# Cross attention over 1601 keys, eight batches: key projection two batches ahead, and the mask of four key tiles added by VectorE

## The chip, the cores and the metric

One Trainium2 chip, one core. The metric is the device time of one execution of the whole kernel in microseconds; the kernel is one launch that computes a four-layer network, and the change touches one function that two of its twelve parts call.

## What is computed

The stream `x` has 8 batches of 64 tokens of width 256; the context has 8 batches of 1601 rows of width 256. Two of the parts are cross attention with 16 heads of width 16, called the second and the fourth here (layers 1 and 3 in the code, tiles `l1x_` and `l3x_`):

```python
def _L1_xattn_ref(queries, keys, values, mask, W_q, W_k, W_v, W_proj, b_proj):
    Q = (queries @ W_q.T).reshape(b, sq, N_HEADS, D_HEAD).transpose(0, 2, 1, 3)   # K, V likewise, of the context
    scores = jnp.einsum('bhqd,bhkd->bhqk', Q, K) / scale
    scores = jnp.where(mask, scores, NEG_INF)
    attention = jax.nn.softmax(scores, axis=-1)
    heads_out = jnp.einsum('bhqk,bhkd->bhqd', attention, V)
    return heads_out.transpose(0, 2, 1, 3).reshape(b, sq, d) @ W_proj.T + b_proj

def _L3_xattn_ref(x, y, attn_bias, Wq, bq, Wk, Wv, Wo, bo, scale_mul_log):
    q = _l2norm(q) * scale_mul
    k = _l2norm(k)
    attn = jnp.einsum('bhqd,bhkd->bhqk', q, k) + attn_bias
    attn = jax.nn.softmax(attn, axis=-1)
    oup = jnp.einsum('bhqk,bhkd->bhqd', attn, v)
    return oup.transpose(0, 2, 1, 3).reshape(B, Lq, C) @ Wo + bo
```

The second has a mask that differs from batch to batch; the fourth has a bias that all batches share, and it normalizes each key's head vector.

## The kernel before

`context_attention` writes five instruction lists, one an engine. After a prologue that prepares batch 0, each engine runs a loop of eight iterations, one a batch. An iteration of batch b walks 13 key tiles (12 of 128 keys and one of 65): on TensorE `turned(b, m)` makes the scores of tile m, keys on partitions, in two banks; ScalarE takes the exponential of both banks (`exp`, L3595) into `pT`; TensorE's `values` (L3448) of the tile before adds up the output. Each tile has two steps, 26 in an iteration, and the list `steps` says which items of other batches' preparation every engine does in which step, between scores and values. The items:

- K (c, j): key projection of channel half c and key piece j (1024 and 577 keys), L3344. In the second, ScalarE makes the high half `kh` (L3530) and VectorE the low half `kl` (L3696). In the fourth ScalarE squares it into `sq` (L3524) and VectorE copies it to `k32` (L3692); `k32` may be written when GpSimd has split the piece of the channel half before.
- N, I, U (fourth only): the sum of squares over a head by TensorE in f32 (L3350) and VectorE's copy (L3707); logarithm and exponential on ScalarE (L3537, L3539); the product with `k32` on VectorE (L3714). Then GpSimd's `split_keys` makes `kh` and `kl` (L3271, L3273).
- V (c): value projection of four key tiles, L3360, and ScalarE's copy into `v33` (L3549).
- A (v, j): scores with queries on partitions of four heads and a quarter of the keys, L3377, from which VectorE takes the masked maxima, two instructions of L3723; 16 a batch. M (c): transposes of the maxima (L3385), put by ScalarE into row 0 of the queries (L3560), so that the scores come out shifted. The scores of a batch begin when both M are in.
- R, E, O, P: the output of the batch before (copy L3571, L3390, division, transposition L3396, projection L3401, addition L3742). O and P stand in every second batch alone.

K, N, V, A, M, E, O and P take turns on two pairs of banks (`slot`), in the order of the list: an item may start on TensorE when the item two before it has been read. `stack` on SP's queue copies `kh` and `kl` by 24 DMAs a batch (L3201) into the rows of `kst`, which has two buffers; A and the scores read it. The context's f32 rows are loaded by SP into one buffer `ctx32`, and split on GpSimd into `ctxh` and `ctxl`, one buffer each, when V of the batch before is done (L3290, L3291).

For tiles whose mask or bias TensorE adds, `turned` begins with one-hot products of 512 columns (L3425): four a tile in the second, eight in the fourth. In the fourth, tiles 0 to 3 (`ON_VECTOR`) have the bias added by VectorE instead (`add_bias`, L3754), from PSUM into `pT`, where the exponential then works in place. For such a tile the next `turned` waits for VectorE's addition, not for the exponential.

In the kernel before, all the items of iteration b, but for R, E, O and P, belong to batch b+1:

```python
    def at_step(b, s):
        of = {"R": b > 0, "E": b > 0, "O": b % 2 == 0 and b > 0, "P": b % 2 == 0 and b > 0}
        return [(it, b - 1 if it[0] in of else b + 1) for it in steps[s] if of.get(it[0], b + 1 < B)]
```

## Time and profile before

| | us |
|---|---|
| median of three runs | 2603.1 (2599.29 to 2604.42) |
| the profiled execution, its own time | 2586.07 |
| its span, first to last instruction | 2584.3 |
| TensorE busy in it | 2251.3 (87%) |
| VectorE, ScalarE, GpSimd busy | 1624.8, 1226.7, 809.8 |
| mean granted clock of TensorE | 0.952 |

The profile shows one execution. A granted clock of 1 is 2.4 GHz and 0.5 is 1.2 GHz; a figure between says how a stretch is shared between the two levels. Durations of single matmuls overlap, since they are pipelined; where a price matters, the distance from start to start is the better one. A wait names the instruction that released it.

### The profile page before, as it was taken

The numbers are of one execution on the slowest core, as the hardware profiler recorded it, in microseconds if no ns is written. First come the engines' busy times: TensorE is split into PE (matmuls) and PEld (weight loads), VectorE is DVE, ScalarE is ACT, GpSimd is POOL, SyncE is SP. The second block draws the span as 40 slices with busy tenths as digits, with TensorE's granted clock in tenths as the row PEclk, the third lists the DMA queues.
The fourth block names the chain that finished last, engine by engine and source line by source line (L and its number), as shares of the span: only waits on it lengthen the run. The fifth ranks groups of instructions, "written<-read, shape, count | busy, mean of one in ns | idle before, by whom it ended". The sixth has DMA issues, their size and how long they took to land. (4 is left out here: it accounts for less than half of the span.)

```text
span 2584.3 us, 63716 instructions
## 1 busy us (share of the span) xinstructions
PE 2251.3 (87%) x26802; PEld 1404.9 (54%) x26810; DVE 1624.8 (63%) x3620; ACT 1226.7 (47%) x2095; POOL 809.8 (31%) x655
## 2 busy tenths in 40 slices
PE   7885788888868899999999998798788888878898
PEld 6753545556534556556566655465345555555554
DVE  6976364544439846888888754545765555554577
ACT  3334144445443235555555554665345544443465
POOL 5610132422207020333322300254544343452154
PEclk9997999999989989999999999899899998888999
DMA  4203343233140256766767651232422222120132
GB/s 115 68 1 94 98 138 98 71 111 94 42 148 19 46 120 134 151 136 128 141 125 143 124 93 46 68 104 88 112 91 66 66 66 66 41 65 22 63 92 64
DMA packets 358542, 229.99 MB, mean 89 GB/s; under 512 B 289817, under 2 KB 325490, under 8 KB 358258
## 3 DMA queue, kind: packets, MB, share of 16 engines
q1 hardware_dynamic: 355186, 217.52, 34.4%
q0 software_dynamic: 3072, 8.39, 1.1%
q8 instruction: 213, 3.49, 0.6%
q14 instruction: 71, 0.58, 0.1%
HBM read 114.02 MB, written 0.52 MB: 44 GB/s over the span
## 5 line engine op out<-in xcount | busy, mean ns | idle before, releaser
L100 PE MATMUL PS<-hot 128*128 128x512 f16 x476 | 140.1, 432 | 82.3 <-DVE l0a_g L1119 17.5
L3960 POOL TENSOR_TENSOR l2x_rows<-l2x_rows,l2x_one 128x256 f16<-128x256 f32 (+1 forms) x91 | 90.9, 1025 | 377.2 <-DVE l2x_rows L1507 352.3
L4064 PE MATMUL PS<-l2x_rows,l2x_pth 128*128 128x512 f16 x832 | 200.4, 379 | 1.5 <-DVE l2x_mean L4273 1.5
L3723 DVE CUSTOM_DVE_ANT_0 l1x_junk<-PS,l1x_bias 128x401 bf16<-128x401 f32 (+1 forms) x256 | 133.1, 575 | 82.3 <-PE PS L3377 82.3
L3723 DVE CUSTOM_DVE_ANT_0 l3x_junk<-PS,l3x_bias 128x401 bf16<-128x401 f32 (+1 forms) x256 | 132.8, 574 | 49.4 <-PE PS L3377 49.2
L3595 ACT ACTIVATE l1x_pT<-PS 128x512 f32<-128x512 f32 (+1 forms) x208 | 112.7, 593 | 98.1 <-PE PS L3431 98.0
L3595 ACT ACTIVATE l3x_pT<-PS 128x512 f32<-128x512 f32 x144 | 77.8, 591 | 171.4 <-PE PS L3431 171.4
L4266 DVE TENSOR_TENSOR l2x_pl<-l2x_sc,l2x_ph 128x1664 f16<-128x1664 f32 x64 | 124.7, 1949 | 44.0 <-ACT l2x_ph L4143 43.4
L4251 DVE CUSTOM_DVE_ANT_0 l2x_sc<-PS,l2x_bias 128x1665 f32<-128x1665 f32 x64 | 120.9, 1889 | 36.3 <-issue 35.1
L4161 ACT ACTIVATE l2x_meanT<-PS 128x256 f32<-128x256 f32 x64 | 24.5, 383 | 249.8 <-PE PS L4026 249.8
L4018 PE MATMUL PS<-l2x_kh,l2x_qth 128*128 128x512 f16 (+1 forms) x512 | 132.0, 339 | 1.5 <-issue 1.5
L4018 PE MATMUL PS<-l2x_kh,l2x_qtl 128*128 128x512 f16 (+1 forms) x512 | 132.0, 339 | 0.0
L4018 PE MATMUL PS<-l2x_kl,l2x_qth 128*128 128x512 f16 (+1 forms) x512 | 132.0, 339 | 0.0
L100 PEld LDWEIGHTS PS<-hot 128*128 128x128 f16 x476 | 45.5, 107 | 154.0 <-issue 45.1
L4064 PEld LDWEIGHTS PS<-l2x_rows,l2x_pth 128*128 128x128 f16 x832 | 79.5, 98 | 72.5 <-issue 2.7
L4136 ACT ACTIVATE l2x_sc<-l2x_sc,l2x_shift 128x1665 f32<-128x1665 f32 x64 | 107.9, 1686 | 19.4 <-DVE l2x_shift L4253 19.4
L4069 PE MATMUL PS<-l2x_rows,l2x_ptl 128*128 128x256 f16 x832 | 111.6, 273 | 0.0
L4143 ACT ACTIVATE l2x_ph<-l2x_sc 128x1664 f16<-128x1664 f32 x64 | 101.8, 1591 | 8.5 <-DMA l2x_pth<-l2x_ph 6.7
L1642 POOL TENSOR_TENSOR l2f_unit_l<-l2f_unit,l2f_unit_h 128x384 f16<-128x384 f32 x72 | 75.0, 1062 | 70.5 <-ACT l2f_unit L1634 70.5
L3696 DVE SCALAR_TENSOR_TENSOR l1x_kl<-PS,l1x_kh 128x1024 f16<-128x1024 f32 (+1 forms) x32 | 31.8, 993 | 101.7 <-ACT l1x_kh L3530 101.6
L1642 POOL TENSOR_TENSOR l3f_unit_l<-l3f_unit,l3f_unit_h 128x384 f16<-128x384 f32 x68 | 73.4, 1101 | 69.7 <-ACT l3f_unit L1634 69.7
L3377 PE MATMUL PS<-l3x_kst,l3x_qst 64*64 64x401 f16 (+1 forms) x512 | 47.6, 386 | 53.5 <-DMA l3x_kst<-l3x_kh 23.4
(865 smaller groups left out, 6038.8 us busy)
## 6 DMA issues: line engine op xcount, KB each, us to landing
l2f_unit<-in_L_ffn_units_dram SPq DMA_DIRECT2D x36, 384.0 KB, 3.0
l3f_unit<-in_L_ffn_units_dram SPq DMA_DIRECT2D x34, 384.0 KB, 3.1
l1x_kst<-l1x_kh SPq DMA_DIRECT2D x128, 100.1 KB, 2.4
l3x_kst<-l3x_kh SPq DMA_DIRECT2D x128, 100.1 KB, 2.4
l2x_rows<-in_ctx_dram SPq DMA_DIRECT2D x8, 1536.0 KB
l1x_ctx<-in_ctx_t_dram SPq DMA_DIRECT2D x7, 1601.0 KB, 7.3
l3x_ctx<-in_ctx_t_dram SPq DMA_DIRECT2D x7, 1601.0 KB, 7.7
l1x_kst<-l1x_kl SPq DMA_DIRECT2D x64, 100.1 KB, 2.5
```

What stands on the lines that cost most here:

```text
L100: self.nc.tensor.matmul(self.PS[:, bank, :], self.hot[:, 0:P], self.hot[:], start=True, stop=True)
L1642: last = self.k.nc.gpsimd.tensor_tensor(wl[:, at], w[:, at], wh[:, at], ALU.subtract)
L3595: nc.scalar.activation(to, of, ACT.Exp, scale=1.0 / S_SCALE).then_inc(exp_done, 1)
L3723: last = v.tensor_tensor_reduce(junk[:, slot(it), r * BANK:r * BANK + n], PS[:, 2 * slot(it) + r, 0:n], bias[:, 0 if normed else b % 2, at ...
L3960: last = nc.gpsimd.tensor_tensor(high[:, at], of[:, at], one[0:p, at].unsqueeze(2).unsqueeze(3).to_broadcast([p, i, NC, P]), ALU.mult)
L4018: last = nc.tensor.matmul(PS[:, j, 0:n], x[:, d, r, :], y[:, b % 2, d, at:at + n], start=(e == 0), stop=(e == len(terms) - 1))
L4064: nc.tensor.matmul(PS[:, ACC, :], pth[:, u % 2, m, :], rows2[:, b % 2, :, :, m, :], start=(m == 0), stop=False)
L4069: last = nc.tensor.matmul(PS[:, ACC, 0:D], ptl[:, u % 2, m, :], rows2[:, b % 2, 0, :, m, :], start=False, stop=(m == KT - 1))
L4136: nc.scalar.activation(sc[:], sc[:], ACT.Exp, bias=shift[:, u % 2:u % 2 + 1], scale=1.0 / S_SCALE, accum_out=rsum[:, u % 4:u % 4 + 1]).the ...
L4143: nc.scalar.activation(ph[:], sc[:, 0:ODD], ACT.Copy).then_inc(p_high, 1)
L4251: link(v.tensor_tensor_reduce(sc[:], PS[:, 0:len(cols), :].rearrange("p b n -> p (b n)")[:, 0:KEYS], bias[:], 1.0, LOWEST, ALU.add, ALU.ma ...
L4266: v.tensor_tensor(pl[:], sc[:, 0:ODD], ph[:], ALU.subtract).then_inc(p_low, 1)
```

## The change

The steps are written anew for both layers. V now stands first, A follows, and K (with N, I and U) comes from step 14 on and belongs to batch b+2, so that keys are stacked an iteration before they are asked for. Iteration 0 has lists of its own (`opening_steps`, `second_keys`): there batch 1 is prepared as before and the keys of batch 2 as well. SP's order of stacking, context and mask loads follows; the context is split in two pieces of keys, so that K of the first piece needn't wait for the second. In the second layer tiles 0 to 3 are added to `ON_VECTOR`: a second mask with keys on partitions is loaded (from a host copy in that layout, 832 bytes a partition), turned into 0 and a large negative number by GpSimd, and added by VectorE.

```diff
--- before.py
+++ after.py
@@ -3010,7 +3010,7 @@
     NEAR = 4.0
     MASKED = -2.0 ** 30
     ONE_HOT = 2.0 ** 6 if normed else 1.0
-    ON_VECTOR = list(range(4)) if normed else []
+    ON_VECTOR = list(range(4))
 
     def vector_count(b, m, g):
 
@@ -3021,29 +3021,45 @@
 
     A = [("A", v, j) for v in range(QV) for j in range(NCH)]
     R_, E, O_, P_ = ("R", 0, 0), ("E", 0, 0), ("O", 0, 0), ("P", 0, 0)
+    K_ = [("K", c, j) for c in range(NC) for j in range(NH)]
+    N_ = [("N", c, j) for c in range(NC) for j in range(NH)]
+    I_ = [("I", c, j) for c in range(NC) for j in range(NH)]
+    U_ = [("U", c, j) for c in range(NC) for j in range(NH)]
+    V_ = [("V", c, 0) for c in range(NV)]
+    M_ = [("M", c, 0) for c in range(2)]
     if normed:
-        steps = [[("K", 0, 0)], [("K", 0, 1)], [("N", 0, 0), R_], [("N", 0, 1), ("I", 0, 0)], [("U", 0, 0), ("I", 0, 1), ("V", 0, 0)],
-                 [E, ("U", 0, 1)], [("V", 1, 0)], [("K", 1, 0)], [("K", 1, 1)],
-                 [O_, ("N", 1, 0)], [("N", 1, 1), ("I", 1, 0)], [("U", 1, 0), ("I", 1, 1), ("V", 2, 0)],
-                 [P_, A[0], ("U", 1, 1)], [A[1], A[2]], [("V", 3, 0)], [A[3], A[4]], [A[5]], [A[6]], [A[7], A[8]],
-                 [A[9]], [("M", 0, 0), A[10]], [A[11]], [A[12], A[13]], [A[14], A[15]], [("M", 1, 0)], []]
+        steps = [[V_[0]], [], [R_, V_[1]], [], [E], [V_[2]], [V_[3]], [O_], [A[0]], [A[1], A[2]], [A[3]], [A[4]], [P_, A[5]], [A[6], A[7]],
+                 [K_[0]], [K_[1], A[8]], [N_[0], M_[0]], [N_[1], I_[0], A[9]], [U_[0], I_[1], A[10]], [U_[1], K_[2], A[11]],
+                 [K_[3], A[12]], [N_[2], A[13]], [N_[3], I_[2], A[14], A[15]], [U_[2], I_[3]], [U_[3]], [M_[1]]]
+        opening_steps = [[K_[0]], [K_[1]], [N_[0]], [N_[1], I_[0]], [U_[0], I_[1], V_[0]], [U_[1], K_[2]], [K_[3], V_[1]], [N_[2]],
+                         [N_[3], I_[2], V_[2]], [U_[2], I_[3]], [U_[3], V_[3]], [], [], [], [], [],
+                         [A[0], A[1]], [A[2], A[3]], [A[4]], [A[5], A[6]], [A[7], A[8]], [A[9], A[10]], [M_[0], A[11]],
+                         [A[12], A[13]], [A[14], A[15]], [M_[1]]]
+        second_keys = {18: [K_[0]], 19: [K_[1]], 20: [N_[0]], 21: [N_[1], I_[0]], 22: [U_[0], I_[1], K_[2]], 23: [U_[1], K_[3]],
+                       24: [N_[2]], 25: [N_[3], I_[2], U_[2], I_[3], U_[3]]}
     else:
-        steps = [[("K", 0, 0)], [], [("K", 0, 1), R_], [("K", 1, 0)], [E], [("K", 1, 1)], [("V", 0, 0)], [O_], [A[0]], [A[1]],
-                 [("V", 1, 0), A[2]], [A[3]], [P_, A[4]], [("V", 2, 0), A[5]], [A[6]], [A[7]], [("V", 3, 0), A[8]], [A[9]],
-                 [("M", 0, 0), A[10]], [A[11]], [A[12]], [A[13]], [A[14]], [A[15]], [("M", 1, 0)], []]
+        steps = [[V_[0]], [], [R_], [V_[1]], [E], [V_[2]], [V_[3], A[0]], [O_, A[1]], [A[2], A[3]], [A[4]], [A[5]], [A[6]], [P_, A[7]],
+                 [A[8]], [K_[0]], [A[9], M_[0]], [A[10]], [K_[1]], [A[11]], [A[12]], [K_[2]], [A[13]], [A[14]], [A[15], K_[3]], [],
+                 [M_[1]]]
+        opening_steps = [[K_[0]], [], [K_[1]], [K_[2]], [], [K_[3]], [V_[0]], [], [V_[1]], [], [V_[2]], [V_[3]], [], [A[0]], [A[1], A[2]],
+                         [A[3], A[4]], [A[5], A[6]], [A[7], A[8]], [A[9], A[10]], [M_[0], A[11]], [], [A[12]], [A[13]], [A[14]], [A[15]],
+                         [M_[1]]]
+        second_keys = {20: [K_[0]], 22: [K_[1]], 23: [K_[2]], 25: [K_[3]]}
-    assert len(steps) == STEPS
+    assert len(steps) == len(opening_steps) == STEPS
     WARM = 3
     OFF_SLOT = "IUQTRFZY"
 
     def at_step(b, s):
-        of = {"R": b > 0, "E": b > 0, "O": b % 2 == 0 and b > 0, "P": b % 2 == 0 and b > 0}
-        return [(it, b - 1 if it[0] in of else b + 1) for it in steps[s] if of.get(it[0], b + 1 < B)]
+        if b == 0:
+            return [(it, 2) for it in second_keys.get(s, [])] + [(it, 1) for it in opening_steps[s]]
+        of = {"R": b - 1, "E": b - 1, "O": b - 1, "P": b - 1, "K": b + 2, "N": b + 2, "I": b + 2, "U": b + 2}
+        return [(it, of.get(it[0], b + 1)) for it in steps[s] if of.get(it[0], b + 1) < B and (it[0] not in "OP" or b % 2 == 0)]
 
     prepared = [(it, 0) for it in first]
     tail = [(R_, B - 1), (E, B - 1), (O_, B - 1), (P_, B - 1)]
@@ -3101,8 +3117,7 @@
         kst = sb("kst", [P, 2, R, NK], F16)
         v33 = sb("v33", [P, 2, KT, H, VW])
         bias = sb("bias", [P, 1 if normed else 2, NK], BF16)
-        if normed:
-            bias_t = sb("bias_t", [P, len(ON_VECTOR), S])
+        bias_t = sb("bias_t", [P, 1, len(ON_VECTOR), S]) if normed else sb("bias_t", [P, 2, KT, S], BF16)
         one_hot = sb("one_hot", [P, BANK], F16 if normed else BF16)
         junk = sb("junk", [P, 2, BANKS], BF16)
         rmax = sb("rmax", [P, 2, QV, NCH])
@@ -3137,6 +3152,7 @@
             q_scale = sb("q_scale", [P, H])
         else:
             mask8 = sb("mask8", [P, NK], U8)
+            mask_t = sb("mask_t", [P, KT, S], U8)
             every = sb("every", [P, NT, NK], U8)
             alive = sb("alive", [P, NT])
 
...
@@ -3189,6 +3205,7 @@
                     for half in range(2):
                         sp.dma_start(mask8[half * S:(half + 1) * S, :],
                                      ins["mask_Bx1xSxS2_bk0"][b].rearrange("a s n -> (a s) n")).then_inc(bias_loaded, 16)
+                    sp.dma_start(mask_t[:], ins["mask_columns"][b]).then_inc(bias_loaded, 16)
 
                 def stack(b, c):
 
@@ -3205,18 +3222,28 @@
                     load_mask(0)
                 sp.dma_start(w[:, 3, :, :], ins[L + weight["o"] + "_heads"].rearrange("g p n -> p g n")).then_inc(loaded["rest"], 16)
                 sp.dma_start(b_o[:], row(ins[L + ("bo" if normed else "b_proj")]).to_broadcast([P, D])).then_inc(loaded["rest"], 16)
-                for b in range(B):
-                    if b + 1 < B:
-
-                        sp.wait_ge(ctx_parts, FIRST_CTX + b)
-                        sp.dma_start(ctx32[:], ins["ctx_t"][b + 1].rearrange("(c p) n -> p c n", p=P)).then_inc(ctx_loaded, 16)
-                        if not normed:
-                            sp.wait_ge(bias_made, b + 1)
-                            load_mask(b + 1)
-                    stack(b, 0)
-                    stack(b, 1)
+                def load_ctx(b):
+
+                    sp.wait_ge(ctx_parts, FIRST_CTX + NH * (b - 1))
+                    sp.dma_start(ctx32[:], ins["ctx_t"][b].rearrange("(c p) n -> p c n", p=P)).then_inc(ctx_loaded, 16)
+
+                load_ctx(1)
+                for c in range(NC):
+                    stack(0, c)
+                if not normed:
+                    sp.wait_ge(bias_made, 1)
+                    load_mask(1)
+                load_ctx(2)
+                for b in range(B - 1):
+                    for c in range(NC):
+                        stack(b + 1, c)
+                    if b + 2 < B and not normed:
+                        sp.wait_ge(bias_made, b + 2)
+                        load_mask(b + 2)
+                    if b + 3 < B:
+                        load_ctx(b + 3)
                 if later is not None:
-                    sp.wait_ge(ctx_parts, FIRST_CTX + B - 1)
+                    sp.wait_ge(ctx_parts, FIRST_CTX + NH * (B - 1))
                     later.load(sp)
 
             @block.gpsimd
@@ -3256,8 +3283,10 @@
                     pool.wait_ge(bias_loaded, (b + 1) * BIAS_LOADS)
                     if b >= 2:
                         pool.wait_ge(turned_made, (b - 1) * STEPS)
+                        pool.wait_ge(biased, vector_count(b - 1, 0, 0))
                     hold()
-                    nc.gpsimd.tensor_scalar(bias[:, b % 2, :], mask8[:], -MASKED, MASKED, ALU.mult, ALU.add).then_inc(bias_made, 1)
+                    link(nc.gpsimd.tensor_scalar(bias[:, b % 2, :], mask8[:], -MASKED, MASKED, ALU.mult, ALU.add))
+                    nc.gpsimd.tensor_scalar(bias_t[:, b % 2, :, :], mask_t[:], -MASKED, MASKED, ALU.mult, ALU.add).then_inc(bias_made, 1)
                     pool.wait_ge(bias_made, b + 1)
 
                 def split_keys(b):
@@ -3287,9 +3316,12 @@
                     pool.wait_ge(ctx_loaded, b * 16)
                     pool.wait_ge(made, number[(LAST_USE, b - 1)] + 1)
                     hold()
-                    link(nc.gpsimd.tensor_tensor(ctxh[:], ctx32[:], one[:].unsqueeze(2).to_broadcast([P, NC, NK]), ALU.mult))
-                    nc.gpsimd.tensor_tensor(ctxl[:], ctx32[:], ctxh[:], ALU.subtract).then_inc(ctx_parts, 1)
-                    pool.wait_ge(ctx_parts, FIRST_CTX + b)
+                    for h, (at, n) in enumerate(halves):
+                        link(nc.gpsimd.tensor_tensor(ctxh[:, :, at:at + n], ctx32[:, :, at:at + n],
+                                                     one[:].unsqueeze(2).to_broadcast([P, NC, n]), ALU.mult))
+                        nc.gpsimd.tensor_tensor(ctxl[:, :, at:at + n], ctx32[:, :, at:at + n], ctxh[:, :, at:at + n],
+                                                ALU.subtract).then_inc(ctx_parts, 1)
+                        pool.wait_ge(ctx_parts, FIRST_CTX + NH * (b - 1) + h + 1)
                     if normed:
                         split_keys(b)
                     else:
@@ -3337,7 +3369,7 @@
                             pe.wait_ge(w_parts, 1)
                             pe.wait_ge(ctx_parts, j + 1)
                         else:
-                            pe.wait_ge(ctx_parts, FIRST_CTX + b)
+                            pe.wait_ge(ctx_parts, FIRST_CTX + NH * (b - 1) + j + 1)
                         for i, at, n in pieces(*halves[j]):
                             terms = [(x, y, d) for x, y in ((wh, ctxh), (wh, ctxl), (wl, ctxh)) for d in range(NC)]
                             for m, (x, y, d) in enumerate(terms):
@@ -3750,8 +3782,11 @@
                         dve.wait_ge(summed, e - 2 * G2 + 1)
                     to = pT[0:n, (b * KT + m) % 2, g, :].rearrange("p (u s) -> p u s", s=S)
                     of = PS[0:n, S_BANK + g, :].rearrange("p (u s) -> p u s", s=S)
-                    each = bias_t[0:n, m, :].unsqueeze(1).to_broadcast([n, BANK // S, S])
-                    v.scalar_tensor_tensor(to, each, S_SCALE, of, ALU.mult, ALU.add).then_inc(biased, 1)
+                    each = bias_t[0:n, 0 if normed else b % 2, m, :].unsqueeze(1).to_broadcast([n, BANK // S, S])
+                    if normed:
+                        v.scalar_tensor_tensor(to, each, S_SCALE, of, ALU.mult, ALU.add).then_inc(biased, 1)
+                    else:
+                        v.tensor_tensor(to, of, each, ALU.add).then_inc(biased, 1)
 
                 for it in prepared:
                     item(it)
@@ -4431,6 +4466,7 @@
     a["L3_xattn_scale_mul_log_row"] = a.pop("L3_xattn_scale_mul_log").reshape(H)
     tiled = lambda v: np.ascontiguousarray(np.moveaxis(columns(v), 0, -3).swapaxes(-1, -2))
     a["fside_columns"] = tiled(a["fside_SxS2_0"])
+    a["mask_columns"] = tiled(a["mask_Bx1xSxS2_bk0"][:, 0])
     n = np.arange(D)
     turns = 2.0 * np.pi * (np.outer(n, n) % D) / D
     a["dft_cos"] = np.cos(turns).astype(np.float32)
```

## Rows read from the trace of the kernel before

**Rows 1.** The page, busy time: us, share of the span, instructions.

```profile
PE 2251.3 (87%) x26802; PEld 1404.9 (54%) x26810; DVE 1624.8 (63%) x3620; ACT 1226.7 (47%) x2095; POOL 809.8 (31%) x655
```

**Rows 2.** Windows, second cross attention by iteration: us, busy of each engine, PEclk, DMA.

```profile
373.50:418.50 45.00, 39.80 (x1046) 26.07 (x1046) 21.27 (x74) 23.11 (x45) 12.75 (x5) 1.00 0.23 58
...
661.30:709.60 48.30, 42.19 (x1086) 27.64 (x1086) 22.10 (x77) 23.86 (x49) 0.86 (x1) 1.00 0.22 54
709.60:737.45 27.85, 20.39 (x918) 14.48 (x918) 0.50 (x2) 15.28 (x31) 0.00 (x0) 0.97 0.02 4
sum 363.95, PE 315.04 PEld 205.66 DVE 153.33 ACT 180.35 POOL 81.63; mean PE 39.38 PEld 25.71 DVE 19.17 ACT 22.54 POOL 10.20
```

**Rows 3.** Windows, fourth cross attention by iteration, same columns.

```profile
1879.70:1938.70 59.00, 49.41 (x1070) 30.39 (x1074) 34.64 (x90) 29.80 (x52) 26.00 (x15) 0.93 0.32 98
...
2249.30:2314.00 64.70, 54.10 (x1135) 32.62 (x1130) 36.36 (x93) 30.78 (x56) 20.56 (x13) 0.90 0.23 65
2314.00:2345.70 31.70, 24.94 (x962) 17.86 (x954) 5.55 (x10) 16.04 (x32) 15.03 (x3) 0.82 0.02 4
sum 466.00, PE 388.30 PEld 240.10 DVE 254.70 ACT 228.64 POOL 190.74; mean PE 48.54 PEld 30.01 DVE 31.84 ACT 28.58 POOL 23.84
```

**Rows 4.** Waits from 1880 to 2345: total us, times, longest.

```profile
PE PS L3377 <- DMA l3x_kst<-l3x_kh: 23.4, 7, 4.0
```

**Rows 5.** Timeline of TensorE, fourth: start, us, what, idle before it.

```profile
2046.00 0.54 PE L3377 MATMUL PS<-l3x_kst,l3x_qst 64*64 64x401 f16 x8 [2.46 <-DMA l3x_kst<-l3x_kh]
2046.47 0.92 PE L3448 MATMUL PS<-l3x_pT,l3x_v 128*17 128x64 f32 x32
```

**Rows 6.** Windows, ten microseconds of a later batch of the fourth.

```profile
2170.00:2180.00 10.00, 8.03 (x170) 4.20 (x170) 5.28 (x21) 2.99 (x7) 5.26 (x1) 0.51 0.58 180
```

**Rows 7.** Timeline of TensorE, second: a key tile with V between.

```profile
482.17 0.41 PE L3425 MATMUL PS<-l1x_one_hot,l1x_bias 64*64 64x512 bf16 x4
482.41 0.42 PE L3431 MATMUL PS<-l1x_qst,l1x_kst 64*64 64x64 f16 x32
...
485.40 0.38 PE L3396 MATMUL PS<-ident,l1x_o 128*128 128x128 f32 x2
485.71 0.64 PE L3448 MATMUL PS<-l1x_pT,l1x_v 128*17 128x64 f32 x32
```

**Rows 8.** Timelines of TensorE, ScalarE and VectorE, second: K and its copies.

```profile
469.39 0.61 PE L3344 MATMUL PS<-l1x_ctxh,l1x_wh 128*128 128x512 f16 x2
...
472.20 1.02 ACT L3530 ACTIVATE l1x_kh<-PS 128x1024 f16<-128x1024 f32 x1 [1.60 <-PE PS L3344]
...
473.25 1.23 DVE L3696 SCALAR_TENSOR_TENSOR l1x_kl<-PS,l1x_kh 128x1024 f16<-128x1024 f32 x1 [7.89 <-ACT l1x_kh L3530]
```

**Rows 9.** Groups from 1830 to 2360: VectorE's maxima and mask additions.

```profile
L3723 DVE CUSTOM_DVE_ANT_0 l3x_junk<-PS,l3x_bias 128x401 bf16<-128x401 f32 (+1 forms) x256 | 132.8, 574 | 49.4 <-PE PS L3377 49.2
...
L3754 DVE SCALAR_TENSOR_TENSOR l3x_pT<-l3x_bias_t,PS 128x512 f32<-128x512 f32 x64 | 41.0, 681 | 42.5 <-PE PS L3431 42.5
```

**Rows 10.** Timeline of TensorE, fourth: the norm products of a channel half.

```profile
2005.44 3.01 PE L3350 MATMUL PS<-l3x_sq,l3x_ones 128*128 128x512 f32 x8
```

**Rows 11.** Timelines of GpSimd and VectorE, fourth: a split and the product beside it.

```profile
2012.40 1.88 POOL L3271 TENSOR_TENSOR l3x_kh<-l3x_k,l3x_one 128x1024 f16<-128x1024 f32 x1
2014.36 2.54 POOL L3273 TENSOR_TENSOR l3x_kl<-l3x_k,l3x_kh 128x1024 f16<-128x1024 f32 x1
...
2013.23 1.67 DVE L3714 TENSOR_TENSOR l3x_k<-l3x_k,l3x_n 128x577 f32<-128x577 f32 x1 [0.32 <-ACT l3x_n L3539]
```

**Rows 12.** Timeline of TensorE, second: scores of the last, partial tile.

```profile
513.04 2.21 PE L3431 MATMUL PS<-l1x_qst,l1x_kst 64*64 64x64 f16 x32
```

**Rows 13.** Timeline of TensorE, fourth, last iteration: two tiles in a row.

```profile
2327.83 0.63 PE L3425 MATMUL PS<-l3x_one_hot,l3x_fsp 64*64 64x512 f16 x8 [0.62 <-ACT l3x_pT L3595]
...
2329.90 0.63 PE L3425 MATMUL PS<-l3x_one_hot,l3x_fsp 64*64 64x512 f16 x8 [0.62 <-ACT l3x_pT L3595]
```

**Rows 14.** Timeline of SP's queue, fourth: issues of stacking DMAs.

```profile
2020.83 1.24 SPq L3201 DMA_DIRECT2D l3x_kst<-l3x_kh  x2
```

4 lines of the change are left out of this document (2 added, 2 removed).

## The prediction

> **What bounds it now.** I read the page first: TensorE is busy for 87% of the span [rows 1], so an edit pays where TensorE stands still or runs at its lower clock. The change touches two layers of the same function, the second cross attention ("second": no key norm) and the fourth ("fourth": with it). I cut both loops into iterations, one per batch, at the ScalarE copy of the row maxima (L3560) that ends each. The second takes 363.95 us for eight iterations, the fourth 466.0 [rows 2, 3]: together a third of the kernel. In the second, iterations 1 to 5 (the sum less the first and the last two) are 363.95 - 45.0 - 48.3 - 27.85 = 242.8 us (48.6 each), TensorE busy 42 of 48 in the one shown, at the full clock. In the fourth they are 466.0 - 59.0 - 64.7 - 31.7 = 310.6 (62.1 each), TensorE busy 49 to 54 in the rows shown, the granted clock 0.90 to 0.93 there and 0.82 in the last.
>
> Then the waits of TensorE. Only the fourth has a big one: score products (L3377) waiting for the key rows that SP's DMAs stack, 23.4 us in 7 waits, one a batch [rows 4]. Its surroundings are as important: it ends at 2046.00, and the values products behind it take 0.92 us where the same 32 take 0.64 at the full clock [rows 5, 7]; in another batch the same phase has a stretch granted 0.51 [rows 6], almost all 1.2 GHz. By the granted clock an iteration spends 2 x (1 - clock) of its time at 1.2 GHz: 0.14, 0.20 and 0.36 in the iterations shown [rows 3]. The second layer has no DMA wait and hardly any of this.
>
> **The change, part by part.** Prices, all by start to start in the timelines: a key tile's scores are 0.24 (bias products, L3425) + 0.35 in the second [rows 7]; V 2.64 us [rows 7]; K of 1024 keys 2.7, its copy on ScalarE 1.0, its low half on VectorE 1.25, so K's pair of banks is free 2.5 us after K ends [rows 8]; a mask addition on VectorE 0.68, a chunk of maxima (A) two of 0.57, which in the timeline start 0.5 apart, so 1.0 an A [rows 9]; the norm product N of a channel half 3.0 [rows 10]; GpSimd's split of a 1024-key piece 4.6, of 577 keys in proportion 2.6; VectorE's 577-wide product beside it 1.67 [rows 11]; the last, partial tile 2.8 to 3.4, as its 1-row weights take 2.2 us [rows 12]; a tile with nothing between its parts 2.07 [rows 13]; the issue of a stacking DMA 0.6 [rows 14]. With these I walk each instruction list in order, each engine in order, each item waiting for the release of its bank pair two items before. Check of the method: the old steps 0 to 5 of the second come out at 13.1 us; the rows give 482.17 - (469.39 - 0.59) = 13.4 [rows 7, 8]. It is 1 to 2% short.
>
> *Mask on VectorE (second only).* Per batch 4 tiles lose 16 bias products, 4 x 0.24 = 1.0 us of TensorE. VectorE gets 8 additions, 8 x 0.65 = 5.2 us, on 22 busy of 48: there is room. But ScalarE's exponentials start one addition later, and the V copy queued behind them in tile 3 too. GpSimd makes a second mask of 832 columns (under the 1.88 us that 1024 columns take [rows 11]) at the start of an iteration, where it idles, and SP issues one more DMA of 0.6: covered, and worth no more than that if uncovered.
>
> *Steps rearranged, second.* V in steps 0 to 6, A0 at 6, K from 14. Ends of tiles, from the iteration's start: tile 3 at 15.5, tile 6 at 23.6, tile 9 at 35.0, tile 11 at 44.8, tile 12 and the maxima at 49.5; without the output items (odd batches) 47.8. TensorE's waits in it: O behind V3's late copy 1.8; M0, which has K0's banks, 2.2 (2.5 less A9's 0.3); A14 behind K2 0.95; A15 0.6; K3 0.7; the copy of the maxima 1.9. Taking 1% on, 5 iterations are 2 x 50 + 3 x 48.3 = 245, with some 3 us of clock 248, against 242.8: +5.
>
> *Ends, second.* Iteration 0 now also makes the keys of batch 2 in steps 20 to 25 (+8.2 us of K, and their waits): the walk gives 54.7 for 45.0. Iteration 6 makes none: 38.8 for 48.3. Zero in sum.
>
> *Steps rearranged, fourth.* The stacking DMAs of batch b+1 no longer follow K by a few steps. They are issued from the end of iteration b-1 (kst is free when batch b-1's scores are done): 12 of 0.6 us [rows 14] for the first half, so heads 0 and 1 are issued at 3.8 and landed by 6.5 us, the last by 17; A0 asks at 13.5, A8 at 29. The DMA wait goes: -3.3 us a batch. On SP only the context load for b+3 stands behind them. But K2's copy on VectorE (step 19) must wait for GpSimd's split of the first piece, since both use k32: U0 ends at 15.5 of the second part, the split at 20.0, K2's copy at 21.2; queued behind K2 on VectorE is A11, and TensorE has nothing it may do, as K3 has K2's banks: an idle of 2.65 us. Before, V and the output items lay there. With 1.2 each before N1 and N2 and 2.0 at the end the second part (steps 14 to 25) is 36.6, the first 23.0 (21.5 in odd batches): 59.6 and 58.1. Five iterations, 1% on: 296.5; at the old rate of clock losses about 307, at full clock 296.5. The A chunks now lie between dense 512-column products, as in the second, where the clock holds; I take 301.5: -9.
>
> *Ends, fourth.* Iteration 0 has both key sets; the second's U0, I1 and K2 stand in one step (22), and K2 waits 4.7 us for GpSimd with A11 behind it: the walk gives 85 for 59.0, +26. Iteration 6 loses 14 us of K and N and all their waits, 40.5 for 64.7: -24. The last one, begun at the low clock before (0.82), -1.5. Sum +0.5, taken as 0 to +1.
>
> Context halves: the same work of GpSimd in two parts. At 4.4 us for 1024 columns [rows 11] it is 9 us for the first half and 14 in all, from V3 at 12 on; K0 asks at 24, K1 at 26.5. Covered, except in iteration 0 of the fourth, where the walk has 1.4 and 1.3 us for it.
>
> **Sum.** Second +5, fourth -9 + 0.5: about -4 us. The profiled execution is 2586.1 (span 2584.3, 1.8 around it), 17 below the median of 2603.1; the sum would make it 2582, and the median 2599. Each walk can be wrong by 1 us a batch either way (10 to 12 us in both layers).
>
> **Rivals.**
> A. *The clock recovers in the fourth.* Its eight iterations spend some 84 us at 1.2 GHz (2 x (1 - clock) x time, added over all eight, of which three are shown [rows 3]); products done in it took twice their time. For: the low stretches follow the DMA wait and the run of small products. Against: a 2.65 us idle takes its place. If it holds the full level, iterations 1 to 5 give 296.5 - 310.6 = -14, the low clock of the old ends -5, the second +5, and 4 of the percents put on go: -18, 2585.
> B. *The wait is exchanged and keeps the clock low (slower).* Place: K3 in step 20, every batch, and 5 us in iteration 0. The old wait of 2.5 us was enough for the lower level [rows 5]; the new one is as long, and behind it stand K3 and N2, 3.4 us of dense work, and the two tiles, which TensorE and not VectorE bounds. At 1.2 GHz that adds 3.5 us, 2.2 more than the 1.3 that I put down for the old stretch [rows 5]; six times +13, the fourth otherwise at its old losses 307 - 310.6 = -4, the second +5: +14, 2617. It decides if the low level follows K3's wait in three or more batches. The Trainium skill (TensorE: Matmul & The Clock Gate, "HAM oscillation") says that a wait recurring in every round of a loop can put the array back to the half clock each round, which speaks against this change if the new wait recurs. By it the time is B's.
> C. *The second layer gains after all.* If the V copies and M0 wait less than walked, the 1.0 us of bias products is kept: -3 in place of +5: 2591. For: its TensorE idles 6 of 48 us, so any order has room. Against: M0 after K0 in the same banks is fixed by the list.
> D. *The transfers stay late:* SP would have to come to stack(b+1) after 10 us, held by the context load that waits for GpSimd. That wait ends at 26 us of the iteration before, so this is unlikely; then the 23.4 us [rows 4] stay beside the new wait, 2622.
>
> **How the numbers follow.** A measurement of this kernel can tell about 0.2%, 5 us, from no change. Forecast 0.36 (2594 to 2604), A 0.24, B 0.22, C 0.14, D 0.04. Faster: A, most of C and 0.06 of the forecast, 0.42. Same: 0.30 and the rest of C, 0.32. Slower: B and D, 0.26. The range holds the forecast with its 10 to 12 us of error, and A and B but for their outer tails: 2578 to 2620.
>
> **What would show it.** Right: no wait of L3377 for the kst DMAs; in the fourth a wait of L3344 of 2 to 3 us in each iteration 1 to 5, released by VectorE's k32 copy (L3692), and that copy's wait now naming GpSimd's split; iterations of 58 to 61 us; iteration 0 over 80, iteration 6 near 40. In the second, a wait before L3385 of about 2 us, iterations of 48 to 50, bias products 288 in place of 416. Wrong: if the granted clock in the fourth is 0.98 (A) or under 0.90 (B), or the second's iterations are at 46 (C).

## The result, and the profile after

| | before | after |
|---|---|---|
| median, us | 2603.4 (2599.29 to 2604.42, 4 runs) | 2637.7 (2625.72 to 2645.39, 4 runs) |
| the profiled execution, and its span | 2586.07, 2584.3 | 2635.16, 2633.4 |
| ratio, 95% interval | | 1.0131 [1.009, 1.0172] |

The change makes the kernel 1.3% slower, 34 us. I had put 2599 first and 2578 to 2620 as the range; the time lies outside it, on the side of rival B, and above B's 2617.

The same windows as in [rows 2] and [rows 3], each from one ScalarE copy of the row maxima to the next. First the second cross attention of the changed kernel (us, busy of each engine, PEclk, DMA share, GB/s):

```profile
389.60:447.90 58.30, 49.39 (x1074) 30.06 (x1078) 29.51 (x88) 26.75 (x48) 14.42 (x8) 0.94 0.30 82
447.90:496.60 48.70, 40.15 (x1084) 26.07 (x1070) 27.14 (x86) 24.07 (x47) 13.53 (x8) 1.00 0.32 90
496.60:547.40 50.80, 41.73 (x1070) 27.21 (x1070) 26.73 (x85) 24.63 (x49) 14.88 (x9) 1.00 0.33 90
547.40:602.70 55.30, 44.48 (x1072) 27.94 (x1064) 26.39 (x84) 24.01 (x46) 14.86 (x9) 0.91 0.29 82
...
654.10:708.10 54.00, 45.33 (x1064) 28.21 (x1064) 26.40 (x84) 24.04 (x47) 14.87 (x9) 0.87 0.21 54
708.10:746.20 38.10, 32.46 (x1022) 22.87 (x1022) 22.63 (x77) 21.23 (x44) 1.81 (x2) 1.00 0.27 68
...
sum 385.60, PE 317.15 PEld 204.84 DVE 191.10 ACT 185.46 POOL 89.34; mean PE 39.64 PEld 25.60 DVE 23.89 ACT 23.18 POOL 11.17
```

and the fourth:

```profile
1915.20:2008.60 93.40, 70.44 (x1146) 39.04 (x1146) 45.46 (x105) 40.23 (x65) 33.07 (x23) 0.89 0.24 68
...
2068.50:2132.70 64.20, 54.47 (x1122) 32.83 (x1122) 35.09 (x93) 31.01 (x57) 26.38 (x18) 0.92 0.24 66
2132.70:2191.10 58.40, 48.99 (x1116) 30.06 (x1116) 34.86 (x92) 30.46 (x54) 26.27 (x18) 1.00 0.26 73
...
2317.60:2363.50 45.90, 39.83 (x1058) 26.31 (x1058) 22.86 (x77) 20.89 (x45) 26.90 (x8) 0.89 0.32 91
2363.50:2394.70 31.20, 23.58 (x938) 16.37 (x938) 5.55 (x10) 15.98 (x31) 0.00 (x0) 0.89 0.01 4
sum 479.50, PE 393.96 PEld 239.00 DVE 251.01 ACT 230.70 POOL 193.74; mean PE 49.25 PEld 29.88 DVE 31.38 ACT 28.84 POOL 24.22
```

Both layers lost: the second 385.6 for 363.95, the fourth 479.5 for 466.0. The iterations differ between executions by a few us, through the clock. Three profiled executions of the changed kernel (two are the controls below) and two of the one before give, us:

| | second before | second after | predicted | fourth before | fourth after | predicted |
|---|---|---|---|---|---|---|
| iteration 0 | 45.0, 45.0 | 58.3, 58.8, 58.3 | 54.7 | 59.0, 58.2 | 93.4, 98.4, 97.4 | 85 |
| 1 to 5, sum | 242.8, 243.7 | 260.2, 260.6, 260.5 | 248 | 310.6, 313.3 | 309.1, 309.5, 306.9 | 301.5 |
| iteration 6 | 48.3, 48.3 | 38.1, 39.6, 40.3 | 38.8 | 64.7, 64.9 | 45.9, 44.2, 46.9 | 40.5 |
| iteration 7 | 27.9, 27.9 | 29.0, 29.7, 29.6 | 27.9 | 31.7, 32.1 | 31.2, 32.6, 31.8 | 30.2 |

By the means: second +13.5 +17.2 -9.0 +1.5 = +23; fourth +37.8 -3.5 -19.1 +0 = +15; together +38, where the medians differ by 34.

One pair of profiles can mislead here by several us. Some kernels of the next section leave one of the two layers in its old form or in its changed one, and their profiles give more executions of each (second, old: the kernel before, h1, e2, f3, f4, g2, g3; changed: the changed kernel, g1, h2, e1; fourth, old: the kernel before, h1, e1, e3, e4, f1, f2, h3; changed: the changed kernel, g1, h2, e2). By the means, the second's loop takes 365.5 us over seven executions of the old form and 389.1 over four of the changed one, +23.6; the fourth's takes 471.6 over eight and 481.0 over four, +9.4. The sum, +33, is that of the medians. By iterations:

| | second before | second after | change | fourth before | fourth after | change |
|---|---|---|---|---|---|---|
| iteration 0 | 45.2 | 58.6 | +13.4 | 59.4 | 96.2 | +36.8 |
| 1 to 5, sum | 241.9 (238.8 to 243.9) | 261.1 (260.2 to 263.2) | +19.2 | 315.3 (310.6 to 318.5) | 307.7 (305.5 to 309.4) | -7.6 |
| iteration 6 | 49.6 | 39.9 | -9.7 | 65.0 | 45.3 | -19.7 |
| iteration 7 | 28.9 | 29.5 | +0.6 | 31.9 | 31.8 | -0.1 |

The waits of TensorE. In the second, iterations 1 to 5 (total us, times, longest):

```profile
PE PS L3417 <- DVE l1x_ticks L3731: 11.0, 5, 2.2
PE PS L3409 <- DVE l1x_rmax L3755: 10.1, 17, 1.0
PE PS L3409 <- DVE l1x_ticks L3731: 6.4, 9, 1.0
```

In the fourth, iterations 1 to 5, and then iteration 0:

```profile
PE PS L3376 <- DVE l3x_k L3724: 14.0, 5, 2.8
PE PS L3409 <- DVE l3x_rmax L3755: 7.4, 10, 1.0
PE PS L3382 <- DVE l3x_ticks L3741: 6.1, 5, 1.2
PE PS L3382 <- DVE l3x_k L3724: 5.7, 5, 1.2
...
PE PS L3409 <- DVE l3x_k L3724: 7.0, 3, 3.6
PE PS L3409 <- DVE l3x_ticks L3741: 2.8, 3, 1.1
PE PS L3376 <- POOL l3x_ctxl L3322: 2.5, 1, 2.5
```

L3417 are M's transposes, L3409 the maxima products, L3376 K, L3382 N, L3724 VectorE's copy to `k32`, L3731 and L3741 its releases of banks behind K and N, L3755 its maxima. The 23.4 us of [rows 4] are gone: no score product waits for a DMA. In their place stands what the prediction named: M0 waits 2.2 us behind K0 in the second, K3 2.8 us behind K2's copy in the fourth, each in every batch. And VectorE's copy itself waits for GpSimd's split (L3302), 15.4 us over the fourth in this row of the groups:

```profile
L3724 DVE TENSOR_SCALAR l3x_k<-PS 128x1024 f32<-128x1024 f32 (+1 forms) x32 | 31.2, 991 | 61.0 <-ACT l3x_sq L3556 45.5 <-POOL l3x_kl L3302 15.4
```

### The profile page after: what moved, and what is told of

Read it like the earlier page. It is cut to its first block and busy times, and to the rows that moved or that the text cites. A ratio compares the mean times of both kernels' runs of the same rounds, so it can differ in the third digit from the quotient of the medians.

```text
span 2633.4 us, 63574 instructions
## 1 busy us (share of the span) xinstructions
PE 2265.6 (86%) x26674; PEld 1403.9 (53%) x26682; DVE 1658.2 (63%) x3684; ACT 1234.6 (47%) x2095; POOL 818.8 (31%) x691
## 5 line engine op out<-in xcount | busy, mean ns | idle before, releaser
L3755 DVE CUSTOM_DVE_ANT_0 l1x_junk<-PS,l1x_bias 128x401 bf16<-128x401 f32 (+1 forms) x256 | 132.1, 574 | 30.2 <-PE PS L3409 29.4
L3755 DVE CUSTOM_DVE_ANT_0 l3x_junk<-PS,l3x_bias 128x401 bf16<-128x401 f32 (+1 forms) x256 | 132.6, 574 | 25.8 <-PE PS L3409 24.6
L3627 ACT ACTIVATE l1x_pT<-PS 128x512 f32<-128x512 f32 x144 | 78.1, 594 | 89.2 <-PE PS L3463 89.0
L4171 ACT ACTIVATE l2x_sc<-l2x_sc,l2x_shift 128x1665 f32<-128x1665 f32 x64 | 107.9, 1686 | 19.5 <-DVE l2x_shift L4288 19.4
L3280 POOL TENSOR_TENSOR l3x_tick<-ones 1x1 f32<-1x1 f32 x39 | 10.9, 281 | 259.0 <-DVE l3x_k L3746 214.0
L4104 PEld LDWEIGHTS PS<-l2x_rows,l2x_ptl 128*128 128x128 f16 x832 | 81.6, 98 | 15.6
```

What stands on the lines that cost most here:

```text
L3627: nc.scalar.activation(to, of, ACT.Exp, scale=1.0 / S_SCALE).then_inc(exp_done, 1)
L3755: last = v.tensor_tensor_reduce(junk[:, slot(it), r * BANK:r * BANK + n], PS[:, 2 * slot(it) + r, 0:n], bias[:, 0 if normed else b % 2, at ...
L4104: last = nc.tensor.matmul(PS[:, ACC, 0:D], ptl[:, u % 2, m, :], rows2[:, b % 2, 0, :, m, :], start=False, stop=(m == KT - 1))
L4171: nc.scalar.activation(sc[:], sc[:], ACT.Exp, bias=shift[:, u % 2:u % 2 + 1], scale=1.0 / S_SCALE, accum_out=rsum[:, u % 4:u % 4 + 1]).the ...
```

## The experiments

The two layers share one function, so each can have its own copy of it. Each was timed in five rounds, `h1` and `h2` in three, against the kernel before on the same chip.

**One layer at a time, one part of the second at a time.** `e1_second_only` has the changed function in the second layer and the old one in the fourth, `e2_fourth_only` the reverse. `e3_mask_only` is the kernel before but for the second's mask on VectorE (`ON_VECTOR`, `bias_t`, `mask_t`), `e4_second_steps` has the second's new lists, context halves and DMA order, without that mask.

> The second layer as after the change, the fourth as before. Theory W (waits written into the new lists, made larger by the lower clock): the second's loop takes 386 us in place of 364, its five middle iterations 51 to 55 where TensorE's clock falls, and the kernel is 18 to 24 us slower than before. Rival P (the loss is not of the lists: 16 us of the profiled difference lie in the first layer, where nothing was changed, in gaps of TensorE that no wait explains): the second's loop still takes 386, but whether the kernel is 20 or 36 us slower depends on whether those gaps in the first layer come with this program too. Rival M (VectorE's mask additions are what costs): as W here; the mask-only kernel parts them.

> The fourth layer as after the change, the second as before. Theory W: the fourth's loop takes about 480 us in place of 466, all of it in iteration 0 (93 for 59) less what iteration 6 gives back (46 for 65), so the kernel is 10 to 15 us slower. Rival P: the loop's time in the timed runs is equal to before, and what differs lies in the first layer.

> The old lists and order of loads; in the second layer alone the mask of key tiles 0 to 3 by VectorE. Theory W: 1 us a batch less on TensorE (32 groups of four bias products, 0.24 us each, 8 us in all), part of it lost to the later exponentials: 0 to 8 us faster than before. Rival M: the longer chain of scores, addition, exponential costs 1 to 2 us in each batch, 8 to 16 us slower.

> The second layer with the new lists and order of loads, its whole mask by TensorE as before; the fourth as before. Theory W: 18 to 30 us slower, as the second-only kernel or some us more, since the lists carry the loss. Rival M: no slower than before by more than 5 us.

| | median, us | ratio, 95% interval | changed loop, us |
|---|---|---|---|
| e1_second_only | 2614.56 | 1.0090 [1.0066, 1.0113] | second 393.2 |
| e2_fourth_only | 2595.11 | 1.0027 [1.0009, 1.0045] | fourth 477.0 |
| e3_mask_only | 2593.09 | 1.0004 [0.9988, 1.0020] | second 368.2 |
| e4_second_steps | 2610.65 | 1.0080 [1.0062, 1.0098] | second 384.5 |

The kernel before had 2590.94 here. The second layer is the larger loss, 23.6 us, the fourth 4 to 7 (less than the 10 to 15 I expected); together 1.0117, inside the whole change's interval. In the second the loss is in the new order of steps (1.0080 of 1.0090): the mask alone neither gives nor takes, though it removes 128 bias products, some 8 us of TensorE by my price. So rival C had nothing to keep: that gain doesn't show with the old order either.

**The controls.** In its profiled execution the changed kernel came to the second's loop 16 us later than the kernel before (389.6 for 373.5), with idles of TensorE in the first layer that no code of the change touches:

```profile
41.55 0.58 PE L423 MATMUL PS<-l0x_w_kvh,l0x_rh 128*128 128x256 f16 x2 [5.20 <-issue]
```

Is it the program or the occasion (all that was measured together, on one chip)? `g1_control` is the changed kernel again; `h1_before_again` and `h2_after_again` are both kernels, unaltered, on one chip.

> The changed kernel again, nothing altered. Its profiled run lost some 16 us in the first layer, in gaps of TensorE that the profile calls issue, before either changed loop. If that belongs to the program, the second's loop starts again at 388 to 391 us and the two halves alone (+0.9% and +0.27%) fall short of the whole: ratio 1.015 to 1.018. If it belongs to that one execution, the loop starts at 371 to 378, the span is near 2615, and the ratio is the sum of the halves, 1.0117 (1.009 to 1.014).

> The kernel before, unaltered, with a profile, on the same occasion as the next run. In some profiled runs, whatever the kernel's first layer, TensorE loses 13 to 16 us before 60 us; the occasions that show it have the kernel before at 2603 and 2607 us, those that don't at 2591 and 2592. If the loss goes with the occasion, both runs of this pair show the second's loop start at the same time, 371 to 378 or 385 to 392. If it goes with the program, this one starts at 371 to 378 and the next at 388 to 392. Ratio 1.000 (0.998 to 1.002).

> The changed kernel, unaltered, beside the kernel before on the same occasion. By the occasion theory its second loop starts where that of the run before starts, within 3 us, and the ratio is 1.012 to 1.015. By the program theory it starts 13 to 16 us later than the run before, at 388 to 392.

g1: 2644.77, ratio 1.0145 [1.0121, 1.0169], its second loop from 391.1; that is the start I expected if the loss was the program's, and a ratio between my two expectations. h1: 2606.83, 1.0004 [0.9983, 1.0024]. h2: 2639.91, 1.0127 [1.009, 1.0164]. The windows from 20 to 60 us, first the profiled kernel before, then h1, then h2:

```profile
20.00:60.00 40.00, 36.94 (x292) 30.05 (x291) 26.92 (x48) 14.94 (x32) 31.50 (x30) 0.93 0.33 95
```

```profile
20.00:60.00 40.00, 30.02 (x197) 21.16 (x195) 18.21 (x31) 9.99 (x21) 29.84 (x29) 0.83 0.32 91
```

```profile
20.00:60.00 40.00, 27.38 (x168) 18.25 (x167) 16.20 (x29) 8.42 (x17) 28.80 (x29) 0.78 0.33 94
```

The kernel before, unaltered, gets through 197 matmuls there instead of 292 and comes to the second's loop at 385.1 instead of 373.5. So most of the 16 us belongs to the occasion. h2 starts 7.3 us later still, at 392.4, where I had asked for 3; but two programs that are the old one up to that loop (g2 and g3 below) start at 391.8 and 385.7 on such an occasion. Whether a part of these 7 us is the program's stays open. The occasion explains the kernel before too: it had 2603 beside the first profile of the changed kernel (389.6) and 2607 in both groups (g, h) whose profiled kernels start at 385 to 392, 2591 and 2592 in both (e, f) whose kernels start at 371 to 378; its first profile, 2586 and 17 below its own median, is of the early kind. Each of the groups e, f, g and h was measured on a chip of its own, so these runs can't tell the chip from the occasion. Each ratio is taken on one chip and hardly feels it: the changed kernel has 1.0131, 1.0145 and 1.0127 where profiles start late, and its two halves, measured where they start early, add up to 1.0117.

**The second: wait or clock?** e1's iterations 1 to 5 are granted 0.88 to 0.97 and take 263.2 us. Three kernels go out from e1. `f1_keys_end_tile` puts M0 ahead of K0, so that it doesn't wait for K0's banks, and one more item of maxima, A13, ahead of K2:

```diff
-[A[8]], [K_[0]], [A[9], M_[0]], [A[10]], [K_[1]], [A[11]], [A[12]], [K_[2]], [A[13]], [A[14]],
+[A[8]], [A[9]], [M_[0], K_[0]], [A[10]], [K_[1]], [A[11]], [A[12]], [A[13]], [K_[2]], [A[14]],
```

`f2_dense_in_maxima` adds idle-filling products, whose result nobody reads, ahead of A0 to A7:

```diff
+                        if b > 0 and c < 2:
+                            k.warm(bank, 2)
```

`h3_spread_values` moves V3 in among the maxima, packs K closer and, as f1, puts M0 ahead of K0:

```diff
-[E], [V_[2]], [V_[3], A[0]], [O_, A[1]], [A[2], A[3]], [A[4]], [A[5]], [A[6]], [P_, A[7]], [A[8]], [K_[0]], [A[9], M_[0]], ...
+[E], [], [V_[2], A[0]], [O_, A[1]], [A[2]], [V_[3], A[3]], [A[4]], [A[5]], [P_, A[6]], [A[7]], [A[8]], [A[9]], [M_[0], K_[0]], ...
```

> As the second-only kernel (0.9% slower than before), but in the second's steps 14 to 23 K stands last in its tile: A9 and then M0, K0; A12, A13 and then K2. Theory W (the waits written into the list are part of the loss): the 2.2 us wait of the maxima transposes behind K0 and the 1.0 of A14 behind K2 go, 2 to 3 us in each of iterations 1 to 5, and the low clock at 30 us of the iteration with them: 10 to 18 us less than the second-only kernel, 0.2 to 0.5% slower than before. Rival C (the clock in the run of small products is the loss, these waits are not): less than 5 us gained.

> As the second-only kernel, with two products of 128x512 that nothing reads put in front of each of the first eight chunks of maxima in the second's loop (into the chunk's own bank, which it then overwrites): 3.5 us a batch more work for TensorE. Rival C (TensorE falls to 1.2 GHz in the run of small products that waits for VectorE, and pays for it in the dense work that follows): the clock stays at its full level at 15 to 24 us of the iterations and the loop is 3 to 10 us shorter, or at least no longer, in spite of 24 us of added products. Theory W (only the waits themselves): the added products fill VectorE's time at best, the loop stays within 3 us, and is up to 15 us longer if they do not fit.

> The second layer's change alone, with values products V3 moved in among the first maxima (step 9) and the keys packed closer (steps 16, 18, 20, 23, with M0 ahead of K0). Theory that the lower clock in the bare run of maxima is what the walk missed: time at the lower clock in iterations 1 to 5 falls from 28 to 36 us to under 20, and these iterations take 247 to 252, ratio 1.001 to 1.004. Rival, the maxima wait for VectorE whatever lies between them, and the order only moves the wait: idle of TensorE stays at 41 to 45, iterations 255 to 260, ratio 1.005 to 1.008.

Iterations 1 to 5 of the second. Idle is the length less TensorE's busy time, and at 1.2 GHz is 2 x (1 - clock) x length, added up:

| | ratio, 95% interval | length | busy | idle | at 1.2 GHz |
|---|---|---|---|---|---|
| before, h1 | 1, 1.0004 | 242.8, 243.7 | 212.7, 214.1 | 30.1, 29.6 | 13.8, 17.1 |
| changed, three times | 1.0131, 1.0145, 1.0127 | 260.2, 260.6, 260.5 | 214.5, 216.9, 216.5 | 45.7, 43.7, 44.0 | 27, 34, 31 |
| e1 | 1.0090 [1.0066, 1.0113] | 263.2 | 219.1 | 44.1 | 36 |
| f1 | 1.0050 [1.0028, 1.0072] | 254.9 | 213.2 | 41.7 | 31.1 |
| f2 | 1.0134 [1.0113, 1.0156] | 262.9 | 227.2 | 35.7 | 7.5 |
| h3 | 1.0078 [1.0053, 1.0103] | 253.1 | 209.9 | 43.2 | 9.2 |

f2, then h3, in two of their windows:

```profile
482.20:536.40 54.20, 46.98 (x1086) 28.91 (x1086) 27.09 (x85) 24.70 (x49) 14.89 (x9) 0.97 0.30 84
536.40:587.90 51.50, 44.28 (x1080) 27.14 (x1080) 26.68 (x84) 24.07 (x47) 14.91 (x9) 1.00 0.32 89
```

```profile
449.30:498.70 49.40, 40.74 (x1083) 26.31 (x1069) 27.36 (x86) 23.88 (x46) 13.45 (x8) 1.00 0.32 89
498.70:549.40 50.70, 42.21 (x1070) 27.13 (x1070) 26.91 (x85) 24.47 (x48) 14.84 (x9) 1.00 0.32 90
```

In these profiles both restore the clock and neither restores the time. f2 pays for it in products: in its profile the iterations take 262.9 us for e1's 263.2. That profile is f2's fastest execution, 2613.87 at a clock of 0.953; the other four had 0.940 to 0.952 and took 2618 to 2629, so the 7.5 us are not those of the ratio, 1.0134. Either way filling the idle is no cure. h3 brings the time at 1.2 GHz under that of the kernel before and keeps the idle at 43.2 us: the clock theory had the time of the low stretches right (under 20) and the length wrong (253 for 247 to 252; 1.0078 for at most 1.004), the rival the idle right (41 to 45). What is left at the full clock is waits. M0's and A14's are a real part: f1, which moves both, takes 8.3 us off e1's iterations 1 to 5 (263.2 to 254.9) and 0.4% off the time. Which of the two gives it was not parted, and the low clock, which I expected to go with them, stays (31 us for 36). M0's wait goes and others take some of its place: K waits 13.2 us there for VectorE (L3755, L3731), 3.0 in the changed kernel.

**The fourth.** Two kernels go out from e2. `f3_second_half_later` moves K2 and K3 one step later, behind A12 and A13, and with them N2 and N3, so that GpSimd has split the first piece by then; `f4_opening` spreads the maxima of iteration 0 from step 13 on instead of 16 and puts K2 and K3 of the second key set into step 24.

```diff
-[U_[1], K_[2], A[11]], [K_[3], A[12]], [N_[2], A[13]], [N_[3], I_[2], A[14], A[15]], [U_[2], I_[3]], [U_[3]], [M_[1]]
+[U_[1], A[11]], [A[12], K_[2]], [A[13], K_[3]], [N_[2], A[14]], [N_[3], I_[2], A[15]], [U_[2], I_[3]], [U_[3], M_[1]]
```

Two more take K2's wait for GpSimd away by a second buffer, in the space of `xn` and `xnT`, which nobody reads any more: `g2_k32_twice` is e2 with it, `g3_k32_twice_opening` f4 with it. `g4_both_amended` is the whole change, with f1's order in the second and g3's fourth.

```diff
-            k32 = sb("k32", [P, NK])
+            k32_both = sb("k32", [P, NK]), x_both
...
+                            k32 = k32_both[c if b > 0 else 0]
                             if x >= NH:
-                                dve.wait_ge(key_low, x - NH + 1)
+                                back = NH if b == 0 or (b == 1 and c == 0) else NC * NH
+                                dve.wait_ge(key_low, x - back + 1)
```

> As the fourth-only kernel (0.27% slower than before), but K of the second channel half comes one to two steps later in the steady iterations (steps 20 and 21, N in 22 and 23), after more chunks of maxima. Theory W (VectorE's copy of K2 waits for GpSimd's split, and K3 waits for it, 2.8 us in each of five iterations): that wait falls under 1 us, 1.5 to 3 us less in each of iterations 1 to 5, 8 to 14 us in all, so 0.1 to 0.3% faster than before. Rival E (the wait only moves to N2, N3 and the end of the iteration): within 4 us of the fourth-only kernel.

> As the fourth-only kernel, but in iteration 0 the chunks of maxima begin at step 13 in place of 16, and the second key set's K2 and K3 stand in step 24, two steps after U0, in place of 22 and 23. Theory W (iteration 0 pays for two key sets with waits of TensorE of 3.6, 2.5, 2.2 and 2.1 us for k32 and for the context split): 5 to 10 us less in iteration 0 (95.5 in the fourth-only kernel), the rest the same, so about equal to before. Rival E: iteration 0 stays over 92, the waits going to N2 and N3 in the last step.

> The fourth layer's change alone, with a second k32 (in the space of xn and xnT, free by then), so that the unit keys of the second channel half do not wait for GpSimd's split of the first. Theory of the exchanged wait: the idle before K3 (2.8 us, iterations 1 to 5) and the 4.5 us in iteration 0 go, 12 to 18 us less than the fourth's change alone: ratio 0.996 to 0.998, iterations 1 to 5 at 58 to 59. Rival, the run of small products and not the wait holds the lower clock and VectorE and ScalarE are next in line: K2's squares on ScalarE and the norm products bring their own waits, 3 to 6 us less, ratio 1.000 to 1.002.

> As the run before, with the order of iteration 0 in which the maxima are spread from step 13 and K2, K3 of the second key set share step 24. The opening order alone was worth 0.3% with one k32. If its gain was the same wait for GpSimd, the two do not add up: ratio within 0.001 of the run before. If it was the spreading of the maxima, they add: another 3 to 8 us, ratio 0.993 to 0.996.

> The whole change with all three amendments: second layer with the key products at the ends of tiles, fourth with two k32 and the spread opening. If the layers add up, the ratio is that of the run before plus 0.005: 0.998 to 1.002, against 1.0131 for the change as made. If it is over 1.004, the layers disturb each other.

| | ratio, 95% interval | it. 0 | 1 to 5 | it. 6 | fourth's loop |
|---|---|---|---|---|---|
| e2_fourth_only | 1.0027 [1.0009, 1.0045] | 95.5 | 305.6 | 44.2 | 477.0 |
| f3_second_half_later | 1.0128 [1.0105, 1.0151] | 98.3 | 330.5 | 41.1 | 501.7 |
| f4_opening | 0.9993 [0.9978, 1.0008] | 90.8 | 310.3 | 44.2 | 477.2 |
| g2_k32_twice | 0.9928 [0.9906, 0.9950] | 89.9 | 292.3 | 47.0 | 460.9 |
| g3_k32_twice_opening | 0.9930 [0.9909, 0.9950] | 84.7 | 291.0 | 44.8 | 452.0 |
| g4_both_amended | 0.9996 [0.9978, 1.0015] | 84.2 | 294.2 | 45.5 | 455.4 |

f3 missed widely: 8 to 14 us less was expected, and by the ratios it takes 26 us more than e2. Its waits of K in iterations 1 to 5 are two, not one:

```profile
PE PS L4163 <- DVE l3x_rmax L4542: 12.0, 5, 2.4
PE PS L4169 <- DVE l3x_ticks L4528: 11.7, 10, 1.2
PE PS L4163 <- DVE l3x_k L4511: 10.2, 5, 2.1
```

(K is L4163 here, N L4169.) K2's and K3's waits for the split shrink from 2.8 to 2.1 us a batch, but K2 now follows A12 in the pairs of banks and waits 2.4 for VectorE's maxima, and N2, N3 and U stand on the iteration's end, where N waits 11.7 us for the banks (6.1 in e2) and the scores 9.3 us in five waits that the profile gives no releaser. To move the waiting item added waits.

g2 is the decisive one. The first rows of its waits in iterations 1 to 5 (K is L4165, A L4198, N L4171; `x_both` is the second buffer), and two of its windows:

```profile
PE PS L4198 <- DVE l3x_rmax L4547: 7.4, 10, 1.0
PE PS L4171 <- DVE l3x_x_both L4515: 6.2, 5, 1.2
PE PS L4171 <- DVE l3x_ticks L4532: 6.1, 5, 1.2
PE PS L4165 <- DVE l3x_x_both L4515: 3.5, 5, 0.7
```

```profile
1987.20:2043.60 56.40, 48.99 (x1116) 30.06 (x1116) 37.33 (x93) 30.55 (x55) 28.33 (x19) 1.00 0.18 54
...
2043.60:2103.20 59.60, 51.91 (x1118) 32.21 (x1122) 35.08 (x93) 30.99 (x57) 26.36 (x18) 0.96 0.26 71
```

K3's wait falls from 13.9 us in e2 to 3.5, the five iterations from 305.6 to 292.3 (13.3 less, 2.7 each), iteration 0 by 5.6, and the kernel is 0.7% faster than before. The two ratios differ by 0.0099, 26 us, with intervals of 0.002 each; the layer's loops by 16, in one execution each. I expected 12 to 18 us, ratio 0.996 to 0.998; where the rest of the 26 comes from stays open. f4's opening order takes 4.7 us off iteration 0; its loop as a whole doesn't show it (477.2), the ratio does by 0.3%. With two buffers the ratio doesn't change (0.9930 for 0.9928), while in the profiles iteration 0 is 5.2 us shorter again; the intervals are too wide for 5 us, so whether the opening order's gain was the same wait is not shown. g2 and g3 are the fastest of all; g4 gives back the 0.5 to 0.7% that the new order in the second costs.

## Why the prediction was wrong, step by step

The waits and their sizes were right: no DMA wait; K3 idle 2.8 us in each of five batches (2.65 predicted), released by the copy of `k32`, which waits for GpSimd; M0 2.2 us (2.2); bias products of the second 288. The test of doing without the K3 wait took 10.4 us of wait and 13.3 of time from five iterations.

**The step that failed is the term for the clock.** The prediction walked at the full clock and added the lower clock as "some 3 us" in the second, 5 in the fourth and nothing in the iterations at the ends, on the ground that the second layer has "hardly any of this". Iterations 1 to 5 of the new order measured 12.7 us over their own full-clock time in the second and 12 over the walk in the fourth, and the fourth's iteration 0 spent 21 to 37 us at 1.2 GHz. The old times on the other side of the comparison held such losses too, 6.8 us in the second's iterations 1 to 5, and were set against the walk as they were. Part by part:

**Second, iterations 1 to 5: +5 predicted, +17 measured (+19 over all executions).** At the full clock the walk holds within 1%: iterations granted 1.00 take 48.7 (odd) and 50.8 (even) for 48.3 and 50. But the 242.8 on the other side hold some low clock themselves: at 1.00 the old order takes 46.6 and 48.3 (46.5 and 46.6 in h1, 46.8 and 48.3 in the profile before), which makes 3 x 46.6 + 2 x 48.3 = 236.4. Against it the new order has 3 x 48.7 + 2 x 50.8 = 247.7: +11.3, where the prediction's own 245 against 236.4 would have been +8.6. I had called 48.6 an iteration "at the full clock" from the one window shown, and walked only steps 0 to 5 of the old list, never the whole. The clock is the rest: 260.4 - 247.7 = 12.7 us for 243.2 - 236.4 = 6.8, 6 us more (I had put 3 in all). Two of the old odd iterations at the full clock, from h1 and from the profile before:

```profile
526.50:573.10 46.60, 40.76 (x1080) 26.82 (x1080) 21.77 (x76) 23.48 (x47) 13.64 (x6) 1.00 0.34 97
```

```profile
614.50:661.30 46.80, 40.73 (x1080) 26.80 (x1080) 21.85 (x76) 23.41 (x47) 13.58 (x6) 1.00 0.33 95
```

The low clock lies at the start of iterations, and in iteration 5 also in the run of maxima and about M0's and K3's waits. V0 of iteration 2, at the full clock, and of iteration 3, at 1.2 GHz:

```profile
497.82 0.39 PE L3392 MATMUL PS<-l1x_wh,l1x_ctxh 128*128 128x256 f16 x2
498.05 0.38 PE L3392 MATMUL PS<-l1x_wl,l1x_ctxh 128*128 128x256 f16 x2
...
548.81 0.61 PE L3392 MATMUL PS<-l1x_wh,l1x_ctxh 128*128 128x256 f16 x2
549.21 0.64 PE L3392 MATMUL PS<-l1x_wl,l1x_ctxh 128*128 128x256 f16 x2
```

0.23 us from start to start in the one, 0.40 in the other. Rival C's ground, that any order has room in 6 us of idle, did not hold: a full-clock iteration of the old order idles 5.8 to 6.1 us, one of the new order 8.6 to 9.1, while TensorE's busy time falls by 0.5. Five times 2.8 us more of idle, less five times 0.5 of busy time, are the +11.3.

**Second, ends: 0 predicted, +6.** Iteration 0 took 58.5 for a walked 54.7, at a clock of 0.94 (7 us at 1.2 GHz); iteration 6 came out as walked; iteration 7 is 1.5 longer.

**Fourth, iterations 1 to 5: -9 predicted, -3.5 (-7.6 over all executions).** At the full clock the odd iteration is 58.4, walked 58.7 with the 1%. The term that was mis-sized is the clock: 5 us put down, 308.5 - 296.5 = 12 measured. That the difference is still near -9 over all executions is luck: the 310.6 it was taken from is the lowest of eight, 4.7 under their mean, and the two errors nearly cancel. Rival A has a part of the truth: the time at 1.2 GHz in these five falls from 51 and 62 us to 29 to 36. It doesn't go, and here is where it stays. After K3's wait in iteration 2 and in iteration 3:

```profile
2115.84 0.39 PE L3376 MATMUL PS<-l3x_ctxh,l3x_wh 128*128 128x512 f16 x1 [2.79 <-DVE l3x_k L3724]
```

```profile
2176.73 0.39 PE L3376 MATMUL PS<-l3x_ctxh,l3x_wh 128*128 128x512 f16 x1 [2.79 <-DVE l3x_k L3724]
```

```profile
2117.80:2120.80 3.00, 1.95 (x6) 0.89 (x7) 1.74 (x5) 0.65 (x1) 0.00 (x0) 0.50 0.00 0
2120.80:2123.80 3.00, 3.00 (x19) 0.76 (x21) 0.66 (x1) 0.00 (x0) 0.00 (x0) 0.50 0.00 0
2178.70:2181.70 3.00, 1.77 (x4) 0.68 (x4) 1.75 (x5) 0.38 (x1) 0.00 (x0) 1.00 0.00 0
2181.70:2184.70 3.00, 3.00 (x81) 1.83 (x80) 2.30 (x6) 1.05 (x3) 0.00 (x0) 1.00 0.02 5
```

The same wait of 2.79 us, with the full clock ahead of it and the same products behind it, is followed by 1.2 GHz in one batch and by the full clock in the next. The first four products of N2 there take 3.78 us in the one and 1.98 in the other. Of the 5.8 us between these two iterations the output items of an even batch take 1.5 by the walk; iteration 2 spends 10 us at 1.2 GHz, which is worth up to 5. Rival B supposed that the low level would follow in three or more batches. The five clocks are 0.97, 0.92, 1.00, 0.92 and 0.95, so its price was too high in these five. Its +14 has the right sign by luck: the measured +34 lay in the second layer and in the fourth's iteration 0. Without most of the wait, in g2, the five iterations spend 18 us at 1.2 GHz where e2's spend 22, in one execution each: if the wait is a cause of the low stretches, it is not the main one. The rule weighed there (the Trainium skill, TensorE: Matmul & The Clock Gate, "HAM oscillation") has the half clock come back with the wait in each round; the trace agrees in iteration 2 and not in iteration 3.

**Fourth, ends: +0.5 predicted, +19 measured (+17 over all executions).** This is the other half of the miss. Iteration 0 took 96 (three executions) for 85, iteration 6 45.7 for 40.5. I gave both the walk's times at full clock and subtracted old ones measured at 0.90 to 0.93. Measured, iteration 0 ran at 0.81 to 0.89, which is 21 to 37 us at 1.2 GHz, and iteration 6 at 0.89 to 0.92, 7 to 10 us. If all of that time were products that take twice as long (as N2's above), half of it would be lost: without it iteration 0 would take 80 to 83 and iteration 6 41 to 42, near the walks of 85 and 40.5. This is an estimate; no run shows these iterations at the full clock. The walk of iteration 0 also named the wait for GpSimd behind K2, 4.7 us (3.6 measured), and the two for the context halves (2.5 measured in one); g2 took 5.6 off it.

So one term runs through most of it. The errors in us: second 12 + 4 + 2, fourth 5.5 + 12 + 5 + 1.5: these 42 lie between the sum of -4 and the measured +38. In all the large ones a full-clock walk with too little for the clock was set against times that had the clock's loss in them. The part of the clock is worked out from the granted clock; in the fourth no run of its own tested it. Why the new order meets more of the low clock in the second, and iteration 0 in the fourth, stays open.

Not tried: the new order with keys for one batch ahead only, which would tell what the second key set of iteration 0 costs by itself.

## What to carry to other kernels

- Before a walked schedule is compared with a measured one, walk the old schedule whole with the same prices, or compare with the iterations that were granted 1.00 alone; the clock's loss is then a term of its own on both sides.
- Work moved a batch further ahead is not free at the ends: what the opening iteration gets comes on top of its own work (+37 us in the fourth), and the last ones gave back half (-20).
- One profile of each kernel isn't enough for terms of a few us: the fourth's iterations 1 to 5 took 310.6 to 318.5 us in eight executions of the same code.
- When a wait is exchanged for another at the same place in a loop, ask for the buffer behind the new one. Here one more `k32` of 6.4 KB a partition turned +0.3% into -0.7%; moving the waiting item by a step made it +1.3%.

## What the runs showed of the hardware

- The same idle of TensorE before the same products was followed by 1.2 GHz in one iteration and by 2.4 GHz in the next (2.79 us, above). A single wait of that length doesn't say which.
- Products without use restored the clock in the profiled execution (7.5 us at 1.2 GHz in five iterations for 36 in e1) and left these iterations as long as before (262.9 for 263.2 us); over all executions the kernel was slower, 1.0134 against 1.0090.
- The unaltered kernel came to the second's loop 12 us later on some occasions, in idles of TensorE with no releaser in the trace (the profile's "issue", 6.8 us in 5 in h1), and its median then is 2603 to 2607 for 2591 and 2592. A profile and a median from two occasions can so differ by 17 us. Every group of runs had another chip, so this may belong to the chip.
